# Up and gate products of an FFN by Strassen's method: seven products of 2x2 blocks in place of eight

## The reference

```python
x = fwht(x * SU_ug) / SCALE
x_up = x @ W_up.T * (Wscale_ug[:INTER] * SCALE)      # INTER = 2048
x_gate = x @ W_gate.T * (Wscale_ug[INTER:] * SCALE)
x = jax.nn.silu(x_gate) * x_up
x = fwht(x * SU_dp) / SCALE
x = x @ W_down.T * (Wscale_dp * SCALE)
```

## Time and profile before

| what | value |
|---|---|
| median of 3 runs | 1533.24 us (1529.28 to 1536.93) |
| profiled execution: its time / its span | 1530.52 us / 1528.7 us |
| TensorE busy | 1469.3 us, 96% of the span |
| VectorE / ScalarE / GpSimd busy | 990.4 / 741.2 / 46.0 us |
| mean granted TensorE clock | 0.992 of full |
| last stage (`ffn`) | from about 969 us to the end |

### The profile page before, as it was taken

How to read it: one execution, slowest core, us unless ns; L and a number is a source line. 1 busy time by engine, 2 the same in 40 slices (tenths; PEclk the granted TensorE clock), 3 DMA queues, 4 the chain that set the end, 5 groups by cost and what they waited for, 6 DMA issues and landing times. The chain is left out here.

```text
span 1528.7 us, 25242 instructions
## 1 busy us (share of the span) xinstructions
PE 1469.3 (96%) x10520; PEld 989.0 (65%) x10520; DVE 990.4 (65%) x1540; ACT 741.2 (48%) x908; POOL 46.0 (3%) x66
## 2 busy tenths in 40 slices
PE   5999999899999999999999999999999999999998
PEld 5886333687333677333677333577888888888886
DVE  5854999784999783899793899674333324334333
ACT  4334999334999334899433999422211212122111
POOL 1000000100000100000100000100000000000000
PEclk9999999999999999999999999999999999999999
DMA  8453000555000544000543400531100101000002
GB/s 265 152 183 124 9 10 9 155 167 192 9 9 10 152 133 147 8 10 9 153 126 126 200 10 9 165 153 46 37 31 26 55 0 55 27 27 28 1 28 83
DMA packets 53051, 120.01 MB, mean 79 GB/s; under 512 B 11472, under 2 KB 33248, under 8 KB 48080
## 3 DMA queue, kind: packets, MB, share of 16 engines
q1 hardware_dynamic: 41632, 69.94, 13.3%
q0 software_dynamic: 11312, 48.55, 10.0%
HBM read 81.56 MB, written 36.90 MB: 77 GB/s over the span
## 5 line engine op out<-in xcount | busy, mean ns | idle before, releaser
L929 ACT ACTIVATE cx_probs<-cx_sc,proj_mbias 128x1024 f32<-128x1024 f32 (+1 forms) x416 | 442.4, 1113 | 41.9 <-PE cx_sc L1188 31.3
L1072 DVE TENSOR_SCALAR cx_probs<-cx_probs 128x1024 f32<-128x1024 f32 (+1 forms) x416 | 270.0, 686 | 54.6 <-ACT cx_probs L929 53.0
L1034 DVE TENSOR_TENSOR cx_padd<-cx_probs,cx_probs 128x1024 f32<-128x1024 f32 x192 | 234.2, 1220 | 0.8
L1188 PEld LDWEIGHTS cx_sc<-cx_q,cx_kt 32*128 32x128 f32 (+1 forms) x2496 | 102.4, 182 | 196.7 <-ACT cx_probs L929 179.9
L1201 PE MATMUL cx_acc<-cx_probs,cx_vt 128*32 128x512 f32 (+1 forms) x1664 | 219.0, 598 | 3.7 <-DVE cx_probs L1072 3.7
L1188 PE MATMUL cx_sc<-cx_q,cx_kt 32*128 32x512 f32 (+1 forms) x2496 | 203.5, 428 | 15.2 <-ACT cx_probs L929 11.7
L136 PE MATMUL cx_sc<-proj_wv,proj_cs 128*128 128x512 f32 (+1 forms) x624 | 153.3, 402 | 7.4 <-DVE cx_kt L1017 7.4
L136 PE MATMUL cx_sc<-proj_cs,proj_wk 128*128 128x256 f32 (+1 forms) x1152 | 149.0, 289 | 11.2 <-DVE proj_wk L585 11.2
L136 PEld LDWEIGHTS cx_sc<-proj_cs,proj_wk 128*128 128x128 f32 x1152 | 145.4, 191 | 15.4 <-issue 14.3
L136 PEld LDWEIGHTS cx_sc<-proj_wv,proj_cs 128*128 128x128 f32 (+1 forms) x624 | 115.1, 187 | 38.0 <-DVE cx_kt L1017 7.4
L1213 PE MATMUL cx_tot<-cx_padd,cx_ones 128*32 128x256 f32 x1536 | 120.9, 390 | 0.0
(11 more groups left out here) (241 smaller groups left out, 1664.5 us busy)
## 6 DMA issues: line engine op xcount, KB each, us to landing
proj_raw<-in_ctxT SPq DMA_DIRECT2D x20, 512.0 KB, 4.7
scr_q<-cx_q SPq DMA_DIRECT2D x3, 2048.0 KB, 7.0
cx_wo<-scr_wo POOLq DMA_DIRECT2D x3, 2048.0 KB, 14.9
scr_xs<-cx_xs POOLq DMA_DIRECT2D x3, 2048.0 KB, 8.6
cx_q<-scr_q SPq DMA_DIRECT2D x3, 1536.0 KB, 10.7
cx_qxt<-in_x SPq DMA_DIRECT2D x4, 1024.0 KB, 9.0
scr_wd<-cx_wdhi POOLq DMA_DIRECT2D x4, 1024.0 KB, 6.7
scr_wd<-cx_wdlo POOLq DMA_DIRECT2D x4, 1024.0 KB, 8.3
```

What stands on the lines that cost most here:

```text
L929: nc.scalar.activation(prob(N)[0:r], sc[n % NSC][0:r], ACT.Exp, bias=mbias[0:r, b, t:t + 1], scale=SCALE).then_inc(exp_done, 1)
L1034: nc.vector.tensor_tensor(padd[z][(g * QP + j) % 2][:], prob(2 * i + z)[:], prob(2 * i + 2 + z)[:], ALU.add).then_inc(added[z], 1)
L1072: nc.vector.tensor_scalar(prob(N)[0:r], prob(N)[0:r], LOW, HIGH, ALU.max, ALU.min).then_inc(clip_done, 1)
L1188: last = nc.tensor.matmul(sc[(2 * i + h // 2) % NSC][0:r, h % 2], kt[own, z, c, t * P:t * P + r], q[own, y, c], start=n == 0, stop=n == 2)
```

## The change

Groups 1 to 7 are done in steps. A step n (14 of them, `SU`) is one group and one pair of batches. The pair's rotated inputs, each cut into two halves of the inner dimension, are a 2x2 block matrix, the group's weights (two blocks of 128 columns x two halves) another, and their four result blocks come from seven block products (Winograd's form) in place of eight, for up (w=0) and gate (w=1) each. A block product has two chunks, so 6 matmuls.

- `Sums` holds seven sums of weight blocks per w: four loads by GpSimd (`load`), four sums on VectorE (`add`, 256 elements a partition), one high part on ScalarE and one low part on VectorE of 1792 elements.
- `Turned` holds the sums of the inputs of a pair, made once: eight sums on VectorE (1024 elements), four high and four low parts. Pair 0's are made beside group 0, pair 1's after it.
- Per step and w, the products run in the order 1, 5, 6, 2, 7, 3, 4 into three banks; 6, 7, 4 add onto product 1's bank, 3 onto 5's. ScalarE copies three intermediate states out (`copies`), VectorE adds a bank to each (`sum_of`).
- Down is done by row tiles of a step, 8 of 6 matmuls, one step late: gate products of n, row tiles of n-1, up products of n. The banks are shared: up products use gp[1], yp[2], yp[3], and row tiles yp[2], yp[3], yp[0], yp[1] in turn.
- Two buffers of residual rows in place of four: after each batch SyncE stores the rows to DRAM and loads those of the next batch with that parity. The second buffers of up/gate and down weights go; down's weights are loaded by GpSimd. The loops are unrolled.

```diff
+    ORDER = (1, 5, 6, 2, 7, 3, 4)
+    BANK = {1: 0, 6: 0, 7: 0, 4: 0, 5: 1, 3: 1, 2: 2}
...
+    def add(self, nc, dve, g, w):
+        v = nc.vector
+        base = ((g - 1) * 2 + 1 - w) * self.STEPS
+        dve.wait_ge(self.raw_in[w], g * 4 * 16)
+        v.tensor_tensor(self.raw(w, self.S1), self.raw(w, self.S3), self.raw(w, self.A22), ALU.add).then_inc(self.step, 1)
...
+        part_banks = [[gp[1], yp[2], yp[3]], [up[0], gp[0], up[1]]]
+        row_banks = [yp[2], yp[3], yp[0], yp[1]]
...
+                for g in range(2, GR):
+                    n = (g - 1) * PAIRS - 1
+                    pool.wait_ge(part_done, parts(n, 1, 4))
+                    sums.load(pool, io, g, 1)
+                    pool.wait_ge(part_done, parts(n, 0, 4))
+                    sums.load(pool, io, g, 0)
+                    pool.wait_ge(down_done, downs(n))
+                    load_down(g)
...
+                def copies(n, w):
+
+                    act.wait_ge(hf_done, units(n - 1))
+                    if w == 0:
+                        act.wait_ge(silu_done, units(n))
+                    for k, product in enumerate((1, 5, 6)):
+                        act.wait_ge(part_done, parts(n, w, product))
+                        nc.scalar.activation(kept[k][:], part_banks[w][Sums.BANK[product]][:], ACT.Copy).then_inc(copied, 1)
...
+                turned[1].split_hi(nc, act, 1)
+                for n in range(SU):
+                    gate(n)
+                    if n == 0:
+                        for k in (2, 3, 4):
+                            turned[1].split_hi(nc, act, k)
+                    elif n % PAIRS == 0:
+                        sums.split_hi(nc, act, group_of(n), 0)
+                    elif n < SU - 1:
+                        sums.split_hi(nc, act, group_of(n) + 1, 1)
+                    upper(n)
...
+                    if u == 6:
+                        sums.split_lo(nc, dve, 1, 0)
...
+                def upper(n):
+                    sum_of(n, 0, 0)
+                    weigh(n, 0)
+                    sum_of(n, 0, 1)
+                    weigh(n, 1)
+                    split_lo(n, 0)
+                    sum_of(n, 0, 2)
+                    weigh(n, 2)
+                    split_lo(n, 1)
+                    weigh(n, 3)
+                    split_lo(n, 2)
+                    split_lo(n, 3)
...
+                for k in range(5):
+                    turned[1].add(nc, dve, k)
+                gate(0)
+                accumulate(LAST)
+                for k in range(5, 8):
+                    turned[1].add(nc, dve, k)
+                turned[1].split_lo(nc, dve, 1)
+                upper(0)
+                for k in (2, 3, 4):
+                    turned[1].split_lo(nc, dve, k)
+                for n in range(1, SU):
+                    gate(n)
+                    downs_of(n - 1)
+                    upper(n)
+                downs_of(SU - 1)
...
+                def products(n, w):
+
+                    tu = turned[n % PAIRS]
+                    pe.wait_ge(sums.lo_done[w], group_of(n))
+                    for product in Sums.ORDER:
+                        bank = part_banks[w][Sums.BANK[product]]
+                        if product == 1:
+                            before = units(n - 1, HELD if n or not w else HELD - 1)
+                            if w:
+                                pe.wait_ge(silu_done, before)
+                            pe.wait_ge(hf_done, before)
+                        if product == 5 and w == 0:
+                            pe.wait_ge(y_read, rows(n - 1))
...
+                        if product in (6, 7, 3):
+                            pe.wait_ge(copied, three(n, w, {6: 1, 7: 3, 3: 2}[product]))
+                        if product == 4:
+                            pe.wait_ge(summed, three(n, w, 2))
...
+                products(0, 1)
+                down(7)
+                products(0, 0)
+                for n in range(1, SU):
+                    products(n, 1)
+                    row_tiles(n - 1)
+                    products(n, 0)
+                row_tiles(SU - 1)
```

More of the change, by code:

```diff
@@ L1358, in ffn @@
-        BESIDE = UN - 2
[L1360 to L1374, removed]
+        part_banks = [[gp[1], yp[2], yp[3]], [up[0], gp[0], up[1]]]
@@ new lines, in ffn @@
+        hf = [m.at(f"hf{i}", [P, S], work_at + (2 + i) * S * 4) for i in range(2)]
+        hs = [m.at(f"hs{i}", [P, 2, S], work_at + (2 + i) * 2 * S * 4, F32R) for i in range(2)]
+        held, weighed = ([m.at(f"{name}{i}", [P, 2, S], work_at + i * 2 * S * 4, dt) for i in range(HELD)] for name, dt in (("held", F32R), ("weighed", F32)))
+        ugs, wds, scale = hand.ugs, hand.wds, hand.scale
+        over = hand.ugs_at
+        gates = [m.at(f"gates{i}", [P, S], over + i * S * 4) for i in range(HELD)]
@@ new lines, in ffn, with buffer, group_of, parts @@
+        last_out, wd_in = m.sem("last_out"), m.sem("wd_in")
+        xs_in, x1_in = hand.xs_in + m.sems("xs_in", 1), m.sems("x1_in", 2)
+        BESIDE = UN - 2
+        assert sums_at <= chain.ob_at
+        KEYS = ((0, 0), (1, 1), (0, 1), (1, 0))
+        BATCHES = list(range(B)) + [2 * (n % PAIRS) + z for n in range(SU) for z in (1, 0)]
+        def buffer(u):
+            return 0 if u <= BESIDE else 1
+        def group_of(n):
+            return 1 + n // PAIRS
+        def parts(n, w, product):
+            return (2 * n + 1 - w) * PARTS + Sums.ORDER.index(product) + 1
@@ L1376, in ffn, with three, units, rows @@
+        def three(n, w, k):
+            return (2 * n + 1 - w) * 3 + k
+        def units(n, k=HELD):
+            return UN + n * HELD + k
+        def rows(n, k=ROWS):
+            return B * ST + n * ROWS + k
+        def downs(n, k=ROWS):
+            return UN + n * ROWS + k
         with nc.Block() as block:
@@ L1398, in _ @@
[L1398 to L1407, removed]
+                sp.dma_start(xs[2].bitcast(F32), scr["xs"][2].rearrange("t p c s -> p t c s")).then_inc(xs_in[2], 16)
@@ L1433, in beside @@
                         chain.signs(nc, act, room, LAST)
+                        sums.split_hi(nc, act, 1, 1)
                         chain.rotated_hi(nc, act, room, LAST)
[L1436 to L1453, removed]
@@ new lines, in upper @@
+                def upper(n):
+                    copies(n, 0)
+                    for k in range(HELD):
+                        act.wait_ge(hf_done, units(n, k + 1))
+                        nc.scalar.activation(held[k][:, 0], weighed[k][:, 1], ACT.Copy).then_inc(h_hi, 1)
+                chain.warm_up(nc, act, ACT.Silu)
+                act.wait_ge(hand.wd_in, 32)
+                for u in range(UN):
+                    unit(u)
+                turned[1].split_hi(nc, act, 1)
[9 more added lines that the diff above has]
+                    upper(n)
@@ new lines, in _ @@
+                dve.wait_ge(hand.wd_in, 32)
+                for u in range(UN):
+                    unit(u)
+                dve.wait_ge(xs_in[2], 16)
+                dve.wait_ge(chain.rot_done, B * HC)
+                dve.wait_ge(chain.xs_lo, B * HC)
+                dve.wait_ge(gate_done, UN)
+                for k in range(5):
[4 more added lines that the diff above has]
+                    turned[1].add(nc, dve, k)
```

388 lines of the change are left out of this document (263 added, 125 removed).

## The result

The changed kernel takes **1565.26 us** (median of 4 runs, 1562.88 to 1568.66) against 1531.30 (4 runs, 1529.28 to 1536.93): ratio 1.0219, 95% interval 1.019 to 1.0249, so 2.2% slower. The forecast was 1564 in a range of 1541 to 1574.

What follows compares the result with a forecast made beforehand. TensorE's matmul count and waits bound groups 1 to 7. Terms -38.2 + 33.3 + 12.9 + 0.5 + 2.7 - 1.8 = +9.4, plus clock +16.0 and +5.4, gave +30.8 us on 1533.2: 1564 us, range 1541 to 1574.

Steps and rivals of the forecast that it cites:

- Removed matmuls: Groups 1 to 7: each of 14 steps drops 12 up and gate matmuls at 0.2275 us, -38.2 us.
- Borders: At 13 step borders, gate product 1 waits for VectorE's fourth scaled product, 2.56 us late each time, +33.3 us.
- TensorE slower inside a step: Listed as a way to be wrong: many satisfied waits slow TensorE within the steps; priced at nothing.
- The clock, +16.0 for the borders: Idle TensorE at three in four of 13 borders lowers its clock, taken as 10 falls at 1.6 us each.
- The clock, +5.4 for the long waits: Clock falls behind three long waits (6.5, 4.8 and 3.2 us), in the first step and at the end, 1.8 us each.
- The first step: Waits of 6.5 us (product 6), 1.6 (up product 5) and 4.8 (product 6 again), behind VectorE's and ScalarE's input sums, +12.9 us.
- The end: Last row tiles wait about 3.2 us for VectorE's low halves, against 0.5 before, +2.7 us.
- Costed at nothing: Transfers, including GpSimd's weight loads in steps and the residual rows' swap through DRAM, were priced at zero.
- the clock holds: Rival: the border waits come but TensorE's clock doesn't fall, 1542.6 us; chance 0.11.
- late raw weights: Rival: GpSimd's weight loads in the steps arrive late, 8.4 us on top of the forecast, 1572 us; chance 0.08.
- VectorE keeps pace: Rival: VectorE is never behind, so a border costs 1.21 us, not 2.56, giving 1530.4 us; chance 0.09.
- deciding point: For the rival VectorE keeps pace: with a border of less than 1.42 us the kernel isn't slower.

Runs made afterwards that it cites:

- e7_eighth: e4_both plus six more matmuls per step for each of up and gate, into a bank that product 2 overwrites: 1556.18 us, 1.0162 of the kernel before.
- e4_both: Changed kernel with VectorE's low halves after the last scaled product and without TensorE's hf_done wait before gate product 1 from step 1 on: 1521.35 us, 0.9919 of before.
- e2_fill: Changed kernel with nine useless matmuls on TensorE ahead of each border's wait, into a free bank: 1546.57 us, 1.0084 of the kernel before.
- e8_quarter: Changed kernel storing and loading only one of four row tiles when residual rows swap through DRAM: 1561.79 us, 1.0194 of the kernel before.
- e1_lo_last: Changed kernel with VectorE's four low halves of a step moved behind its last scaled product: 1537.59 us, 1.0023 of the kernel before.
- e3_gate_free: Changed kernel without TensorE's wait on VectorE's fourth scaled product (hf_done) before gate product 1, from step 1 on: 1530.50 us, 0.9986 of the kernel before.
- e5_start: Changed kernel with ScalarE's four high halves of pair 1's sums put behind step 0's copies: 1546.29 us, 1.0087 of the kernel before.

## Why the prediction was right

Sign, size and range held, and the working held in nearly all of its steps.

- **Removed matmuls, -38.2:** shown at 38.4 by the step lengths of e7_eighth against e4_both.
- **Borders, +33.3:** the chain of 6.27 us on VectorE is there to the hundredth. Late by 2.29 us (a step of 32.84 less 30.55), not 2.56, since TensorE's products follow at 1.36 to 1.40 us and not at 1.365. The difference, 0.28 us a step, is the price of "TensorE slower inside a step", which I had put at nothing (what makes a product slower, its waits or its changes of bank and operand, no run separates). The two errors cancel: 32.84 - 30.27 = 2.57 a step.
- **The clock, +16.0 for the borders:** 10 of 13, as assumed, at 1.65 us. e2_fill shows it as a cost apart from the wait. That the count met "three in four" is luck in part: it came from four rows, and e8_quarter, with the same idles, has 9. The sentence that there is no fall below 1.99 us is wrong for the trace of before, which has one behind two idles of 1.20 us (TensorE's timeline, then the stretch behind it, columns as in the earlier trace rows, with a granted clock of 0.50):

```profile
613.25 0.97 PE L1188 MATMUL cx_sc<-cx_q,cx_kt 32*128 32x512 f32 x12 [1.20 <-ACT cx_probs L929]
615.42 1.38 PE L1188 MATMUL cx_sc<-cx_q,cx_kt 32*128 32x512 f32 x12 [1.20 <-ACT cx_probs L929]
...
616.00:619.00 3.00, 3.00 (x20) 0.69 (x20) 2.56 (x5) 2.49 (x3) 0.00 (x0) 0.50 0.03 5
```
- **The clock, +5.4 for the long waits:** two at 2.3 us and the end at 1.34 (12.75 against 11.41), together 5.9.
- **The first step, +12.9:** right sum, wrong parts. Measured in starts of products: 4.98 us for product 6 (1068.07 + 1.40 due, 1074.45 come), 1.34 and 4.45 for the others, 10.8 in all, and about 1.9 for unit 7's wait, which I had overlooked: 12.7. That wait is also most of why product 6 came 4.98 us late and not 6.5: it gave VectorE time for the up sums' low half, which then didn't hold up unit 7's scaled product as forecast (VectorE was idle for 0.97 us ahead of it, at 1064.78).
- **The end, +2.7:** 2.83 us of idle TensorE, forecast 2.8.
- **Costed at nothing:** GpSimd's four issues took 2.81 us (2.8 assumed), VectorE's first weight sum followed the accumulate at 1191.57 without a wait, and the swap lies beside other work (e8_quarter).
- **Missed:** unit 7's wait, as said; a wait of 1.16 us in group 0, VectorE's for the first load of residual rows, at 1000.68, which TensorE didn't feel; and the 6.1 us by which the attention happened to be longer in the profiled execution. The medians differ by 34.0 us, 3.2 more than the sum's 30.8: 1.2 of it is the stage's (32.0 against 30.8), the rest is of the size of the attention's spread. The forecast of 1564 came close because the median of before, then 1533.24, came out 1.9 lower with a fourth run.

Of the rivals, "the clock holds" fell by the 10 rows of half rate; "late raw weights" by the missing wait; "VectorE keeps pace" by the waits of 2.1 to 2.2 us. Its deciding point was right, though: e1_lo_last takes the border's idle to 0.93 to 1.03 us, that is a border of 1.3 to 1.4, and ends within 0.2% of before.

Still open: what decides whether an idle of TensorE near 2 us brings the clock down, and so why a prediction from one trace can only guess the count.

## What to carry to other kernels

An algorithm that trades matmuls for sums moves the bound to the engine that makes the sums, and there to one stretch, not to its average: price the chain behind the last product that the next step needs, in that engine's own order, and put whatever nobody waits for behind it. A wait on TensorE of about 2 us mostly cost nearly twice its length here, and it came once a step: taking out one wait that a later one covers (e3_gate_free, 33.7 us) was worth nearly as much as all the removed matmuls (38.4). The same arithmetic was 2.2% slower or 1.9% faster by the order of operations and two waits.

## What the runs showed of the hardware

- There is no sharp length of idle time at which TensorE's clock falls. In the last stage idles of up to 1.65 us never brought it to half in 11 profiles; 1.84 us did, once (e3_gate_free); 1.93 or 1.94 us in group 0 did in 2 of 11 profiles (e1_lo_last and e7_eighth); 2.11 to 2.29 us at the borders did in 29 of 39 cases (after, e5_start, e8_quarter), for 1.65 us of lost time each; 2.82 or 2.83 us ahead of the last row tiles did in 6 of 9. In the attention two of 1.20 us, 2.17 us apart, came ahead of a fall. Nine matmuls in the gap removed every fall at the borders.
- Which of the 13 held is regular within the last stage: the borders at 1175.51, 1311.98 and 1448.51 in after, every fourth, 1157.06, 1293.58 and 1430.11 in e5_start, and 1101.49, 1238.02, 1374.52 and 1511.04 in e8_quarter, 136.5 us apart in all three. Why is open. In the attention the same idle of 2.18 us went either way in two executions. How often it falls there moves the kernel's time by some 8 us (966.70 to 975.25), more than several effects that one wants to read: compare lengths of a stage, not ends of spans.
- A matmul of 512 columns with its weight load costs 0.2275 us in series (12 in 2.73 us). Where each product of six has another bank and other operands, a product takes 1.36 to 1.41 us, up to 0.045 more than six of them; which of its waits, banks and operands makes the difference is not shown.
